# A graph layer and a mixture of experts on one core: another order of the first stage's steps on VectorE, ScalarE and TensorE

## What is computed

```python
x = x + gnn(layernorm(x), adj, W, a)
x = x + ffn(layernorm(x), Wg, bg, W1, b1, W2, b2)

# gnn: Wh = h @ W; e = leaky_relu(e_src + e_dst.T, 0.2), masked by adj
#      out = elu(softmax(e) @ Wh)
# ffn: gate = x @ Wg.T + bg; the best 2 of 8 experts, softmax over the two
#      y_e = relu(x @ W1[e].T + b1[e]) @ W2[e].T + b2[e]; out = weighted sum of the two
```

## Time and profile before

| what | value |
|---|---|
| median of 3 runs | 505.11 us (505.02 to 507.4) |
| the profiled execution's own time | 506.94 us |
| its span, first to last instruction | 505.1 us |
| mean granted clock of TensorE | 0.871 |
| busy, share of the span: PE, DVE, ACT, POOL | 79%, 74%, 64%, 57% |
| exp of step 1 starts | 17.35 us |
| exp of step 16 starts | 195.25 us |
| due_i, the last line of the first stage | 219.79 us |

### The profile page before, as it was taken

The page is one execution under the profiler, slowest core; times in us unless marked ns, Lnnn a source line. Parts: engine busy times, 40 slices in busy tenths (PEclk is TensorE's granted clock), DMA queues, the critical chain, the costliest instruction groups (busy, mean ns, idle before and its releaser), DMA issues.

```text
span 505.1 us, 9093 instructions
## 1 busy us (share of the span) xinstructions
PE 400.2 (79%) x2030; PEld 313.8 (62%) x2044; DVE 372.2 (74%) x1416; ACT 322.9 (64%) x760; POOL 289.7 (57%) x283
## 2 busy tenths in 40 slices
PE   3868887779877786509999999999999999999000
PEld 2645655667665564407887878778787878888000
DVE  6479999887789877544777777686777777777914
ACT  2568788776777767305777777676776767777000
POOL 0002777666656765765366656666665666566564
PEclk9889999775588769557999999999999999999755
DMA  5585333322222322343223232323223232227987
GB/s 135 163 326 162 94 98 96 90 86 84 78 78 84 90 86 79 94 129 104 64 84 103 81 100 76 96 80 105 79 84 100 84 106 84 74 84 258 346 247 241
DMA packets 55068, 59.73 MB, mean 118 GB/s; under 512 B 7553, under 2 KB 40705, under 8 KB 54785
## 3 DMA queue, kind: packets, MB, share of 16 engines
q1 hardware_dynamic: 36880, 35.41, 23.6%
q0 software_dynamic: 8704, 17.97, 10.8%
q10 hardware_dynamic: 9456, 6.06, 4.0%
HBM read 26.75 MB, written 24.28 MB: 101 GB/s over the span
## 4 chain that ended last, share of the span: by engine, by line
PE 55%; issue 11%; ACT 11%; DVE 9%; POOL 5%; DMA 5%; SPq 1%; ACTq 1%; POOLq 0%; DVEq 0%
PE bank L1189 6%; POOL moe_rows L499 5%; PE bank L1172 5%; PE bank L1176 5%; PE bank L1173 5%; PE bank L1186 5%; PE bank L1187 5%; PE bank L1092 4%; PE bank L1115 3%; ACT xn L617 3%; PE bank L1076 3%; PE bank L1133 3%; PE bank L1153 3%; PE bank L1161 2%; ACT prob L572 2%
## 5 line engine op out<-in xcount | busy, mean ns | idle before, releaser
L486 POOL DMA_INDIRECT expert_slots<-rows,slot_i x128 | 126.3, 987 | 105.3 <-DVE slot_i L771 69.0
L499 POOL DMA_INDIRECT moe_rows<-hrelu,ysi x40 | 43.1, 1076 | 38.4 <-DVE ysi L989 20.2
L999 DVE CAST hh<-z 128x512 fp32r<-128x512 f32 x36 | 18.1, 502 | 58.2 <-ACT z L656 58.2
L1186 PE MATMUL bank<-hh,w_hi 128*128 128x512 f32 x144 | 60.4, 420 | 0.0
L665 ACT ACTIVATE yb<-bank,b_sb 128x512 f32<-128x512 f32 x36 | 24.8, 689 | 54.1 <-PE bank L1189 54.1
L1172 PE MATMUL bank<-xh,w_hi 128*128 128x512 f32 x144 | 58.0, 402 | 0.8 <-ACT xh L642 0.8
L1189 PE MATMUL bank<-hl,w_hi 128*128 128x512 f32 x144 | 58.1, 404 | 0.1
L1176 PE MATMUL bank<-xl,w_hi 128*128 128x512 f32 x144 | 57.5, 399 | 0.0
L1173 PE MATMUL bank<-xh,w_lo 128*128 128x512 f32 x144 | 57.5, 399 | 0.0
L1187 PE MATMUL bank<-hh,w_lo 128*128 128x512 f32 x144 | 56.9, 395 | 0.0
L499 POOL DMA_INDIRECT moe_rows<-u,ysi x32 | 39.1, 1222 | 23.6 <-issue 12.9
(11 more groups left out here) (153 smaller groups left out, 1063.1 us busy)
## 6 DMA issues: line engine op xcount, KB each, us to landing
xs<-expert_slots SPq DMA_DIRECT2D x36, 260.0 KB, 2.7
rows<-xn SPq DMA_DIRECT2D x32, 256.0 KB
x_all<-x SPq DMA_DIRECT2D x16, 256.0 KB, 2.9
w_raw<-w_t SPq DMA_DIRECT2D x2, 2048.0 KB, 12.1
w_raw<-moe_rows SPq DMA_DIRECT2D x16, 256.0 KB, 5.7
out<-x_all ACTq DMA_DIRECT2D x16, 256.0 KB, 3.6
w_hi<-moe_rows SPq DMA_DIRECT2D x9, 256.0 KB, 4.5
expert_slots<-rows,slot_i POOLq DMA_INDIRECT x128
```

The source lines that it names most:

```text
L486: nc.gpsimd.indirect_dma_start(out=slots, out_offset=bass.IndirectOffsetOnAxis(ap=slot_i[q][:, k * SUB + j:k * SUB + j + 1], axis=0), in_= ...
L499: nc.gpsimd.indirect_dma_start(out=moe_rows, out_offset=bass.IndirectOffsetOnAxis(ap=ysi[b][:, t:t + 1], axis=0), in_=ys[b][:, t, :], in_o ...
L1186: nc.tensor.matmul(ps_y[:, :], w2_hi[:, e, c, :], hh[:, c, :], start=c == 0, stop=False)
```

## The change

On ScalarE the high halves move from the end of the step to behind exp, and from steps 7 to 14 to steps 9 to 16 (`HIGH`); Ln and Exp of the variance move ahead of xn1's copy; the copy of wh moves ahead of that of xn2's transposes. On VectorE slot_i moves up behind the bases, then come bn3, u, score and neg_max, x_all's update, bn2, xn1, and only then the aggregates and var2; the low halves move from steps 8 to 15 to steps 10 to 17 (`LOW`). On TensorE the wh matmuls move ahead of xn2's transposes. The loop of `by_steps` covers steps 10 to 13 in place of 8 to 13, on every engine. No instruction is added or taken away but a semaphore's count (`met`).

```diff
--- before.py
+++ after.py
@@ -38,6 +38,7 @@
 MASKED = -1e30
 META = 4
 FIRST = 1
+HIGH, LOW = 9, 10
 
 
 C_IDENT = 0
@@ -338,9 +339,9 @@
             def at(t):
                 step(t, [t - n if 0 <= t - n < GROUPS else None for n in range(STAGES)], t % 2, t // 2)
 
-            for t in range(E):
+            for t in range(LOW):
                 at(t)
-            with eng.Fori(E // 2, GROUPS // 2 - 1) as m:
+            with eng.Fori(LOW // 2, GROUPS // 2 - 1) as m:
                 for q in range(2):
                     step(2 * m + q, [2 * m + (q - n) for n in range(STAGES)], q, m)
             for t in range(GROUPS - 2, GROUPS + STAGES - 1):
@@ -571,11 +572,21 @@
                     for j in range(SUB):
                         nc.scalar.activation(prob[:, j, :], score[:, j, :], ACT.Exp, bias=neg_max[:, j:j + 1],
                                              accum_out=psum_row[:, j:j + 1]).then_inc(exp_ok, 1)
+                if not isinstance(t, int):
+                    high_halves(2 * m + (q - HIGH))
+                elif 0 <= t - HIGH < E:
+                    high_halves(t - HIGH)
                 if g1 is not None:
                     act.wait_ge(prob_ps, g1 + 1)
                     if later(g1):
                         act.wait_ge(av_ps, g1)
                     nc.scalar.copy(prob_t[:, :, :], tiles(ps_tp)).then_inc(prob_t_ok, 1)
+                if gx is not None:
+                    act.wait_ge(var2_ok, gx + 1)
+                    n = norms(gx)
+                    nc.scalar.activation(log2_v[:, 0:n, :], var2[:, 0:n, :], ACT.Ln).then_inc(log2_ok, 1)
+                    act.wait_ge(log2_ok, gx + 1)
+                    nc.scalar.activation(root2[:, 0:n, :], log2_v[:, 0:n, :], ACT.Exp, scale=-0.5).then_inc(root2_ok, 1)
                 if g0 is not None:
                     act.wait_ge(xn1_ps, g0 + 1)
                     if later(g0):
@@ -585,12 +596,6 @@
 
                     act.wait_ge(gap_ok, gl + 1)
                     nc.scalar.activation(gap_e[:, :], gap[:, :], ACT.Exp).then_inc(gape_ok, 1)
-                if gx is not None:
-                    act.wait_ge(var2_ok, gx + 1)
-                    n = norms(gx)
-                    nc.scalar.activation(log2_v[:, 0:n, :], var2[:, 0:n, :], ACT.Ln).then_inc(log2_ok, 1)
-                    act.wait_ge(log2_ok, gx + 1)
-                    nc.scalar.activation(root2[:, 0:n, :], log2_v[:, 0:n, :], ACT.Exp, scale=-0.5).then_inc(root2_ok, 1)
                 if g1 is not None:
 
                     act.wait_ge(av_ps, g1 + 1)
@@ -616,20 +621,16 @@
                     for j in range(SUB):
                         nc.scalar.activation(xn2[q][:, j, :], x_all[:, bass.ds(gx, 1), j, :].rearrange("p g d -> p (g d)"), ACT.Identity, bias=shift[:, j:j + 1],
                                              scale=rstds[:, bass.ds(gx, 1), 0, j]).then_inc(xn2_ok, 1)
+                if g0 is not None:
+                    act.wait_ge(wh_ps, g0 + 1)
+                    nc.scalar.copy(wh[:, :, :], tiles(ps_wh)).then_inc(wh_ok, 1)
                 if gx is not None:
                     act.wait_ge(xn2_ps, gx + 1)
                     if later(gx):
                         act.wait_ge(gate_ps, gx)
                     nc.scalar.copy(xn2_t[:, :], ps_t3[:, :]).then_inc(xn2_t_ok, 1)
-                if g0 is not None:
-                    act.wait_ge(wh_ps, g0 + 1)
-                    nc.scalar.copy(wh[:, :, :], tiles(ps_wh)).then_inc(wh_ok, 1)
                 if isinstance(t, int) and t + 1 < len(BATCHES):
                     first_root(t + 1)
-                if not isinstance(t, int):
-                    high_halves(2 * m + (q - (E - 1)))
-                elif E - 1 <= t < 2 * E - 1:
-                    high_halves(t - (E - 1))
 
             by_steps(act, step)
             act.wait_ge(table_ok, 1)
@@ -727,10 +728,6 @@
                 g0, g1, gx, gl, gr = groups
                 if isinstance(t, int) and t == 0:
                     first_stats(0)
-                if gx is not None and norms(gx) > 1:
-                    dve.wait_ge(x_in[q], 16 * (m + 2))
-                    for j in range(SUB):
-                        nc.vector.bn_stats(bn3[:, j, :], x_all[:, bass.ds(gx + AHEAD, 1), j, :].rearrange("p g d -> p (g d)"))
                 if gr is not None:
 
                     dve.wait_ge(rank_ps, gr + 1)
@@ -749,19 +746,6 @@
                     nc.vector.tensor_tensor(base[:, :, :], count_f[:, bass.ds(gr + 1, 1), :].to_broadcast([P, SUB, E]),
                                             cst[:, C_BASE:C_TOKEN].rearrange("p (t e) -> p t e", t=SUB), ALU.add
                                             ).then_inc(base_ok, 1)
-                if gx is not None:
-
-                    dve.wait_ge(hrelu_ok, gx + 1)
-                    dve.wait_ge(hexp_ok, gx + 1)
-                    nc.vector.scalar_tensor_tensor(u[:, :, :], hrelu[:, :, :], 1.0, hexp[:, :, :], ALU.add, ALU.min
-                                                   ).then_inc(u_ok, 1)
-                if gx is not None:
-
-                    dve.wait_ge(u_ok, gx + 1)
-                    nc.vector.scalar_tensor_tensor(x_all[:, bass.ds(gx, 1), :, :].rearrange("p g s d -> p (g s) d"),
-                                                   u[:, :, :], -1.0,
-                                                   x_all[:, bass.ds(gx, 1), :, :].rearrange("p g s d -> p (g s) d"),
-                                                   ALU.add, ALU.add).then_inc(x2_ok, 1)
                 if gr is not None:
 
                     dve.wait_ge(slotp_ok, gr + 1)
@@ -770,9 +754,16 @@
                     with nc.allow_low_precision(reason="one term of a sum is a slot's number, the others are zero"):
                         nc.vector.tensor_reduce(slot_i[q][:, :], slot_p[:, :, :, :].rearrange("p k t e -> p (k t) e"),
                                                 AX, ALU.add).then_inc(slot_ok, 1)
-                if gx is not None:
-
-                    dve.wait_ge(x2_ok, gx + 1)
+                if gx is not None and norms(gx) > 1:
+                    dve.wait_ge(x_in[q], 16 * (m + 2))
+                    for j in range(SUB):
+                        nc.vector.bn_stats(bn3[:, j, :], x_all[:, bass.ds(gx + AHEAD, 1), j, :].rearrange("p g d -> p (g d)"))
+                if gx is not None:
+
+                    dve.wait_ge(hrelu_ok, gx + 1)
+                    dve.wait_ge(hexp_ok, gx + 1)
+                    nc.vector.scalar_tensor_tensor(u[:, :, :], hrelu[:, :, :], 1.0, hexp[:, :, :], ALU.add, ALU.min
+                                                   ).then_inc(u_ok, 1)
                 if g1 is not None:
 
                     dve.wait_ge(z_ok, g1 + 1)
@@ -782,36 +773,23 @@
 
                     dve.wait_ge(score_ok, g1 + 1)
                     nc.vector.tensor_reduce(neg_max[:, :], score[:, :, :], AX, ALU.max, negate=True).then_inc(neg_ok, 1)
+                if gx is not None:
+
+                    dve.wait_ge(u_ok, gx + 1)
+                    nc.vector.scalar_tensor_tensor(x_all[:, bass.ds(gx, 1), :, :].rearrange("p g s d -> p (g s) d"),
+                                                   u[:, :, :], -1.0,
+                                                   x_all[:, bass.ds(gx, 1), :, :].rearrange("p g s d -> p (g s) d"),
+                                                   ALU.add, ALU.add).then_inc(x2_ok, 1)
+                if gx is not None:
+
+                    dve.wait_ge(x2_ok, gx + 1)
+                    dve.sem_inc(met, 1)
                 for j in range(SUB):
 
                     if gx is not None:
                         last = nc.vector.bn_stats(bn2[:, j, :], x_all[:, bass.ds(gx, 1), j, :].rearrange("p g d -> p (g d)"))
                         if j == SUB - 1:
                             last.then_inc(stats2_ok, 1)
-                if gx is not None:
-
-                    dve.wait_ge(stats2_ok, gx + 1)
-                if gl is not None:
-                    if later(gl):
-                        dve.wait_ge(rowid_ok, gl)
-                        dve.wait_ge(token_ok, gl)
-                    nc.vector.tensor_scalar(token_f[:, :, :], token_f[:, :, :], float(GROUP), None, ALU.add).then_inc(token_ok, 1)
-                if gx is not None:
-                    for j in range(SUB):
-                        last = nc.vector.bn_aggr(mv2[:, j, :], bn2[:, j, :])
-                    if norms(gx) > 1:
-                        for j in range(SUB):
-                            last = nc.vector.bn_aggr(mv3[:, j, :], bn3[:, j, :])
-                    last.then_inc(aggr2_ok, 1)
-                if gx is not None:
-                    dve.wait_ge(aggr2_ok, gx + 1)
-                    last = nc.vector.tensor_scalar(var2[:, 0, :], mv2[:, :, 1], EPS, None, ALU.add)
-                    if norms(gx) > 1:
-                        last = nc.vector.tensor_scalar(var2[:, 1, :], mv3[:, :, 1], EPS, None, ALU.add)
-                    last.then_inc(var2_ok, 1)
-                    if norms(gx) > 1:
```

(81 more changed lines are left out.)

## The result

The changed kernel takes 493.06 us (median of 6 runs, 491.76 to 501.73) against 504.99 for the kernel before (6 runs): a ratio of 0.9752, 95% interval 0.9728 to 0.9776, 12 us less. Forecast were 489.9, range 486.0 to 498.5. The profiled execution took 492.37, its span is 490.5. Now and then an execution of one of these kernels takes 8 to 18 us longer at a lower clock (here the one of 501.73); such runs are in the medians and ranges, not in the ratios.

What follows compares the result with a forecast made beforehand. VectorE was taken to bound short steps, a ScalarE-TensorE-ScalarE round trip, with TensorE partly slow, the long ones. Terms by step sum to -15.2: 505.11 becomes 489.9 us, range 486 to 498.5.

Steps and rivals of the forecast that it cites:

- t up to 2: Steps to t=2: ScalarE's wait for the maximum shrinks, -1.0 us, between -0.7 (neg_max alone) and -1.5 (with xn1).
- t=3 to 6: Four short steps before any halves: 40.92 us becomes 4 x 10.1 = 40.4, -0.5.
- t=7 and 8: Two steps that lose their halves: 11.82 and 12.90 us become 10.1 each, -4.5.
- t=9: Step with high halves only, 0.5 us of them covered: 13.91 us becomes 10.3, -3.6.
- t=10 to 15: Six steps with halves: 77.06 us becomes 6 x 11.8 = 70.8, -6.3.
- Tail: Stage's end: high halves in t=16 add 0.5 us, low halves of t=16 and 17 fall in VectorE's waits; +0.7.
- Sum: All terms together: -15.2 us, 491.7 for a profiled execution, 489.9 for the median.
- Rival C: Gaps before gate and rank lower the clock in short steps too: slower, +5, 510 us; chance 0.06.
- Rival A: Clock stays low, and lower, in steps with halves: 12.5 us each in t=10 to 15, 496.6; chance 0.19.
- rival B: Full clock throughout, VectorE alone bounds: 11.4 us a step with halves, 10.0 for short ones, 487; chance 0.22.
- Rival D: No difference: second stage starts on POOL's rows and SP's copies, cutting the gain at POOL's 25 us slack; chance 0.05.
- The new wait: ScalarE waits for var2 before Ln and Exp: 0 to 0.3 us a step, 4 us in all; taken as 0.

Runs made afterwards that it cites:

- e8: The changed kernel with VectorE's old order, the rest of the change kept: 493.16 us, ratio 0.9749 to the kernel before.
- e11: e9 with wh ahead of xn2's transposes on TensorE and ScalarE, as in the changed kernel: 496.51 us, ratio 0.9822 to the kernel before.
- e7: The changed kernel with xn2's transposes and their copy ahead of wh, as before: 494.29 us, ratio 0.9785 to the kernel before.
- e9: The kernel before with high halves at the end of steps 8 to 15, low in 10 to 17, loop over 10 to 13; old orders: 504.23 us, ratio 0.9995.
- e6: The changed kernel with high halves at the end of the step before, ahead of exp: 492.97 us, ratio 0.9740 to the kernel before.
- e12: The changed kernel with high halves in steps 11 to 18, low in 12 to 17 and after the stage, loop over 12 and 13: 487.71 us, ratio 0.9629.
- e2: The changed kernel with high halves ahead of exp, on a chip where the kernel before took 592.18 us: 566.88 us.

## Why the prediction was right, and where it wasn't

The sign and the range held. By the steps of the sum, profiled execution against profiled execution:

- **t up to 2**, -1.0: measured -1.94 (exp of t=3 at 36.70 for 38.64). Above its upper bound of 1.5. ScalarE's wait for neg_max in t=2 fell to 0.88. VectorE's order is not all of it: with VectorE's old order and wh new exp of t=3 starts at 37.47 (e8) or 37.68 (e11), which is 1.0 to 1.2 under the kernel before. With VectorE's new order and wh old (e7) it starts at 36.47. So here too either can stand in for the other, and I had not counted wh.
- **t=3 to 6**, -0.5: measured +0.4. "10.1 each" failed: 10.33 each. VectorE's own path grew by some 0.2 in the step shown, and the clock fell.
- **t=7 and 8**, -4.5: the two steps are 20.61, -4.1.
- **t=9**, -3.6: 10.60, -3.3.
- **t=10 to 15**, 70.8: measured 70.29. The number was right, the reason for four of the six steps. t=10 to 13 took 46.71, 11.68 each, near VectorE's bound of 11.8 in the loop. For t=14 and 15 the sum took the same 11.8, but they lie behind the loop and have no bn3, so VectorE's path is shorter: e7 and e8 make them in 10.5 each. They took 11.79 each because VectorE waited there for z and hexp. That the whole term came out is in this part luck.
- **Tail**, +0.7: +1.16.
- **Sum**, -15.2: 505.1 less 490.5 is -14.6, all of it ahead of due_i.

The larger miss is the last line: "505.11 - 15.2 = 489.9 for the median". The profiled execution of before lay 1.83 above its median, and that of after lies 0.7 below its own. A sum made within one profiled execution had the scatter of that execution in its terms, and I took the full difference off the median. The medians moved by 12, the profiles by 14.6. e9 shows it again: its stage is 3.9 us shorter than that of the profile before (due_i at 215.86 for 219.79), and its median is the same. Nothing is missing there: 1.2 of the 3.9 come back behind due_i (286.5 us for 285.3), 2.0 are what the profile of before lay above the median of its six runs, and 0.7 is the difference between the two chips' medians of the kernel before.

The attribution was the weak part. I priced high halves and wh as two terms that add, 0.5 and 1.0 a step. The runs showed that each can be taken back for nothing while the others stand (e6, e7, e8), and that all together are worth 11 (changed against e9). In t=10 to 13 the gain ends at VectorE's path, in t=14 and 15 at a new wait for z. The loop's bounds I priced at nothing; e9, in which they move together with the halves, is the same as before within 1.2 to 1.7 us.

Rival C was right in its mechanism and wrong in its price. The granted clock of t=3 to 6 fell to 0.83, under the 0.85 at which I said that it decides. It cost 0.5 us, not 5.9. I had taken the price from a step in which the old waits for wh and for the transposes stood on the path; with these covered the slower av holds VectorE up by little (0.25 us ahead of u in the step shown). What it costs in t=14 and 15 is not shown. Rival A's 12.5 a step did not come, B's 11.4 neither: 11.7. Rival D, that the second stage would start no earlier, did not come: from due_i to the end it is 285.3 us before and after, so all that the stage gained reached the end. But POOL's slack of 25.6 us shrank by more than the gain, since it now waits 8.7 us for slot_i in the whole stage.

The new wait, Ln and Exp ahead of xn1's copy, shows with 0.6 us in t=10 to 15. Its cost was not measured by itself.

Of the signs that the prediction named, these came: due_i at 205.22 (near 205), no wait of ScalarE for wh or for xn2's transposes, TensorE's idle time before gate, POOL's first write of a group 0.47 us after u (65.08) where it was 3.29 (68.64). "10.1 in t=3 to 8" did not. And the clock of t=3 to 6 left 1.00, which it had named as a sign of being wrong; the time hardly followed the clock.

On the clock the trace has more to say than I did. I argued by the longest gap (1.16 was held at 2.4 GHz). The changed kernel has shorter gaps, 0.26 and 0.68, and falls in every short step; e7 has the gap of 1.16 and 0.32 before prob's transposes, and holds 1.00. So in these two orders the longest gap does not decide. The rule cited from the Trainium skill, "TensorE: Matmul & The Clock Gate", Part 1, that activity releases the clock, gave rival B; with the gap filled the order looked denser, and the clock was lower. The measurement decides: that rule did not tell which of two orders of equal work keeps the clock.

What stays open: why t=14 and 15 are slower with both new orders than with either; what stopped the engines on the first chip; and how much of the 3 us of the later steps is the tail's cover and how much the loop's.

## What to carry to other kernels

Waits along one round trip between two engines stand in for one another: price a group of reorderings by the distance to the next bound (here VectorE's own path of a step), not by adding the waits, and test by taking all of them back as well as each. Before pricing a lower clock, ask whether the slowed engine still ends anything. Once one engine's path sets the length, take work off that engine into another stage's idle time (e12), and compare medians with medians: a single profile can lie off its median, here from 4.9 us below (e7) to 2.4 above (e12). And look at the last steps of a pipeline by themselves, since some of the work is no longer in them: a mean over six steps hid that the last two had another bound.

## What was not expected of the hardware

Filling TensorE's gap of 1.16 us and opening one of 0.68 lowered its granted clock from 1.00 to 0.83 in every short step; the reverse edit (e7) restored it, and the same move by itself in the old orders did the same (e9 1.00, e11 0.84). By these two pairs of profiles it cost some 0.5 us in four steps. On one chip the four kernels and the kernel before took 15 to 17% longer; in e2's profile ScalarE stood still for 1 to 4 us at a time from t=4 on, 10 times for xn1's copy alone (28.4 us), with VectorE and TensorE idle in part of these times.
